# Decoder layer with routed experts: the low half of the hidden values is computed on VectorE for the second group's pairs of tiles

## The reference, cut to what matters

```python
shared = _swiglu(xf, sW1, sW2, sW3)
h = silu(einsum('td,efd->etf', xf, eW1)) * einsum('td,efd->etf', xf, eW3)
eo = einsum('etf,edf->etd', h, eW2)
specialist = einsum('te,etd->td', combine, eo)      # combine: two experts of eight per token
moe_out = (shared + specialist).reshape(B, S, d)
```

## Time and profile before

| | |
|---|---|
| median of 3 runs | 2320.03 us (2316.13 to 2321.22) |
| the profiled execution's own time | 2315.4 us |
| its span, first to last instruction | 2313.7 us |
| mean granted TensorE clock | 0.934 |
| busy: PE / DVE / ACT / POOL | 85% / 60% / 52% / 30% |
| experts' part | about 2040 to 2313.7 us |
| second group's pairs beside the gathers | about 2205 to 2282 us |

### The profile page before, as it was taken

One profiled execution on the slowest core, in us unless ns is written; L12 is line 12 of the kernel. 1 busy time (PEld: TensorE's weight loads), 2 busy tenths in 40 slices (PEclk: granted clock), 3 DMA queues, 4 the chain that ended last, 5 costly groups with the idle time before them and its releaser, 6 DMA issues. The chain is left out here.

```text
span 2313.7 us, 37956 instructions
## 1 busy us (share of the span) xinstructions
PE 1958.2 (85%) x13464; PEld 1002.0 (43%) x13464; DVE 1397.7 (60%) x3126; ACT 1194.2 (52%) x2157; POOL 699.9 (30%) x693
## 2 busy tenths in 40 slices
PE   4899999999999999967999999847888887459973
PEld 2556565655565656542333233212333333236642
DVE  5665656564656565526878777735677876513344
ACT  2554545454545454534777777743555664125541
POOL 2111101110111111122333333124466666412266
PEclk8999999999999999987999899977999998779996
DMA  5111111111111021123223222200011201133355
GB/s 155 46 40 34 38 37 37 37 38 38 37 32 43 20 46 29 37 63 57 56 56 56 37 50 55 32 18 28 1 37 38 65 28 37 39 101 104 105 161 155
DMA packets 97082, 122.82 MB, mean 53 GB/s; under 512 B 14305, under 2 KB 73985, under 8 KB 96897
## 3 DMA queue, kind: packets, MB, share of 16 engines
q1 hardware_dynamic: 79872, 93.11, 17.1%
q0 software_dynamic: 6144, 16.79, 2.3%
q10 hardware_dynamic: 10880, 10.49, 1.4%
HBM read 52.64 MB, written 33.82 MB: 37 GB/s over the span
## 5 line engine op out<-in xcount | busy, mean ns | idle before, releaser
L1037 DVE TENSOR_REDUCE x_NM<-x_pm 128x1 f32<-128x512 f32 x512 | 342.6, 687 | 108.4 <-PE x_pm L780 106.3
L962 ACT ACTIVATE x_PR<-x_pS 128x512 f32<-128x512 f32 x512 | 300.9, 601 | 115.6 <-PE x_pS L796 108.9
L309 PE MATMUL a_pa<-a_PR,a_V 128*128 128x512 f32 (+3 forms) x1024 | 340.7, 440 | 0.7 <-ACT a_PR L389 0.3
L389 ACT ACTIVATE a_PR<-a_pS 128x384 f32<-128x384 f32 (+1 forms) x384 | 201.4, 525 | 206.7 <-PE a_pS L298 204.3
L471 DVE CUSTOM_DVE_ANT_0 a_pm<-a_pm,a_causal 128x128 f32<-128x128 f32 (+3 forms) x512 | 247.2, 509 | 84.9 <-PE a_pm L284 70.1
L544 POOL CAST a_YT_hi<-a_Y 128x512 f16<-128x512 f32 x64 | 40.2, 628 | 759.1 <-DVE a_Y L479 759.1
L780 PE MATMUL x_pm<-x_KT,x_QT 48*128 48x512 f16 x512 | 198.6, 406 | 22.7 <-DMA x_QT<-q_k_parts 22.0
L796 PE MATMUL x_pS<-x_QT,x_KT 49*128 49x512 f16 x512 | 194.2, 396 | 17.3 <-ACT x_PR L962 16.1
L479 DVE TENSOR_TENSOR a_Y<-a_pa,a_RS 64x512 f32<-64x512 f32 x128 | 88.0, 688 | 181.0 <-ACT a_RS L397 179.8
L309 PEld LDWEIGHTS a_pa<-a_PR,a_V 128*128 128x128 f32 x1024 | 174.7, 192 | 29.8 <-ACT a_PR L389 11.3
L284 PE MATMUL a_pm<-a_KA,a_QA 128*128 128x128 f16 (+3 forms) x512 | 142.5, 308 | 44.9 <-DVE a_NM L471 27.9
(11 more groups left out here) (360 smaller groups left out, 4519.4 us busy)
## 6 DMA issues: line engine op xcount, KB each, us to landing
a_QA<-a_nat_q SPq DMA_DIRECT2D x128, 128.0 KB, 2.3
e_xr<-sent SPq DMA_DIRECT2D x80, 128.0 KB
made<-e_eo ACTq DMA_DIRECT2D x40, 256.0 KB
a_KA<-a_nat_k SPq DMA_DIRECT2D x64, 128.0 KB, 2.3
a_KB<-a_nat_k SPq DMA_DIRECT2D x64, 128.0 KB, 2.4
x_KT<-q_k_parts SPq DMA_DIRECT2D x48, 128.0 KB, 4.3
x_QT<-q_k_parts SPq DMA_DIRECT2D x48, 128.0 KB, 4.4
f_w_stage<-in_w SPq DMA_DIRECT2D x12, 512.0 KB
```

Of the source, the lines that this page charges most:

```text
L309: m = eng.matmul(pa[j % 2][:, P * kc:T], V[:, u % 2, kc, j, :], PR[:, i % 4, at:at + T - P * kc], start=(kc == 0), stop=(kc == TT - 1))
L389: eng.activation(PR[:, i % 4, 0:n], pS[i % 2][:, 0:n], ACT.Exp, scale=SCALE).then_inc(s_e, 1)
L962: eng.activation(PR[:, kc, j, :], pS[i % 2][:, :], ACT.Exp, scale=SCALE).then_inc(s_e, 1)
L1037: eng.tensor_reduce(NM[:, v % 2, c:c + 1], ring_bank("max", v, n)[:, :], AX.X, ALU.max, negate=True).then_inc(s_red, 1)
```

## The change

In the pairs of the second group (p from 28 to 39) `low` is taken from POOL's loop and put into DVE's, behind `hidden_out(p-1)` and in front of the additions. The first group's 28 pairs keep it on POOL. The waits of `low` and the semaphore it raises stay the same. The functions `side_by_side` and `Plan` are also moved to another place in the file, with no change in them.

```diff
 # vector_program
+        def low(p):
+            eng.wait_ge(s_hi, p + 1)
+            after(eng, s_ht, p - 1)
+            eng.tensor_tensor(H16[1][:, p % 2, :, :], TH[:, p % 2, :, :], H16[0][:, p % 2, :, :], ALU.subtract).then_inc(s_lo, 1)
+
...
                 activate(p)
             if 1 <= p <= NP:
                 hidden_out(p - 1)
+            if firsts[1] <= p < NP:
+                low(p)
             if p >= 2:
                 for i in returns_at(p - 2):
                     combine(i)
 # gpsimd_program
         for p in range(NP + 2):
-            if p < NP:
+            if p < firsts[1]:
                 low(p)
             if p >= 1:
                 for i in returns_at(p - 1):
                     gather(i)
```

More of the change, by code:

```diff
@@ L122, in low, with side_by_side, __init__, work_behind @@
                                  op0=ALU.mult, op1=ALU.subtract).then_inc(self.split_done, 1)
+def side_by_side(*threads):
+    at = [next(t, None) for t in threads]
+    while any(a is not None for a in at):
+        n = min((a, i) for i, a in enumerate(at) if a is not None)[1]
+        at[n] = next(threads[n], None)
+class Plan:
+    HOP = 0.2
+    WEIGHT = 0.01
+    def __init__(self, threads):
+        self.at, ended, free = {}, {}, {}
+        behind = self.work_behind(threads)
+        heads, begun = [0] * len(threads), [0.0] * len(threads)
+        while True:
+            ready = []
+            for i, steps in enumerate(threads):
+                if heads[i] < len(steps):
+                    name, before, passes = steps[heads[i]]
+                    if all(n in ended for n in before):
+                        t = max(begun[i], free.get(passes[0][0], 0.0), *(ended[n] for n in before))
+                        ready.append((t - self.WEIGHT * behind[name], t, i))
+            if not ready:
+                break
+            _, t, i = min(ready)
+            name, before, passes = threads[i][heads[i]]
+            begun[i] = t
+            for e, us in passes:
+                t = max(t, free.get(e, 0.0))
+                self.at.setdefault((e, name), t)
+                free[e] = t + us
+                t += us + self.HOP
+            ended[name] = t
+            heads[i] += 1
+        assert heads == [len(steps) for steps in threads]
+    def work_behind(self, threads):
+        own = {name: sum(us + self.HOP for _, us in passes) for steps in threads for name, _, passes in steps}
+        then = {name: [] for name in own}
+        for steps in threads:
+            for n, (name, before, _) in enumerate(steps):
+                for x in before:
+                    then[x].append((name, own[x]))
+                if n:
+                    then[steps[n - 1][0]].append((name, 0.0))
+        behind = {}
+        for first in own:
+            stack = [first]
+            while stack:
+                rest = [n for n, _ in then[stack[-1]] if n not in behind]
+                if rest:
+                    stack += rest
+                else:
+                    name = stack.pop()
+                    behind[name] = max([own[name]] + [behind[n] + us for n, us in then[name]])
+        return behind
@@ L1228, in cross_attention @@
         block.tensor(tensor_program)
[L1231 to L1295, removed]
 class Stage:
```

## The result

| | before | after |
|---|---|---|
| median, same chip | 2320.34 us (9 executions, 2316.13 to 2331.82) | 2336.1 us (9 executions, 2333.3 to 2348.2) |
| profiled execution's own time | 2315.4 us | 2335.06 us |
| first gather to the end of the span | 103.2 us | 120.3 us |

The ratio of the times is 1.0074, with a 95% interval of 1.005 to 1.0098. Forecast were 2312.8 us and a range of 2306.0 to 2318.5: the result lies outside, on the slow side. Executions of one kernel scatter by some 15 us, most of it upstream of the part that changed (in the traces kept, the first gather starts anywhere between 2201.9 and 2224.5 us).

What follows compares the result with a forecast made beforehand. Bound: the start of group 1's first gather at 2286.23, set by the store of pair 39. Gains 1.2 + 1.3 + 1.7 + 3.0 = 7.2 us took the 2320.03 us median to 2312.8, range 2306.0 to 2318.5.

Steps and rivals of the forecast that it cites:

- The failed step: Pairs beside the gathers: rows_out stays 1.42 us later than in the quiet cycle, so 6.53 us a pair against 6.71.
- (1): Start of the pairs beside the gathers: tanh(32) comes at 2221.9 in place of 2223.08, 1.2 us earlier.
- (2): Seven steps from the tanh of pair 32 to that of pair 39: 6.53 us each instead of 6.71, gaining 1.3 us.
- (3): Last pair: PE can take the low half 3.57 us after tanh instead of 5.28, gaining 1.7 us.
- (4): PE's clock in the last pair: 2.4 GHz through the 6.09 us from transposes to result copy, gaining 3.0 us, or 0.
- The third rival: Beside the gathers: denser gathers make signals to ACT's rows_out later; at 3.1 us lateness 4.6 us slower, 2324.6; chance 0.16.
- the first rival: Beside the gathers: late signals vanish with POOL's low half, steps near 5.15 us; gain 13.3 us, 2306.7 us; chance 0.2.
- The second rival: DVE's low half and POOL's gathers shut each other out; 3.6 us lost, gain only 3.6, 2316.4 us; chance 0.12.
- Its chain in the prediction: DVE's rows_out, high, low, additions, next activate: 6.65 us after tanh; behind a whole gather it passes 7.16 by about 0.45.

Runs made afterwards that it cites:

- e5_again: The changed kernel, unchanged, run again on chip 12 as control; ratio 0.9953 to the kernel before, 2305.73 us against 2318.89.
- e3_both: The kernel before, with VectorE doing the low-half subtraction a second time, into scratch, where the change puts it; chip 12, ratio 1.0015 to the kernel before.
- e1_spacer: The changed kernel plus one 1.16 us scratch subtraction on POOL before each set of gathers; chip 12, ratio 1.0012 to the kernel before.
- e18_fifth: The changed kernel, unchanged, on chip 14 as control; ratio 1.0088 to the kernel before, 118.3 us from first gather to the end.

## Why the prediction was wrong, and where it was right

**The failed step** is the one that I called a choice: the pairs' lateness beside the gathers is "1.42 us more than in the quiet cycle", "I keep its lateness", "since the gathers that go with it stay". The gathers stay in number, but not in density. POOL's low half was also the pause between them, and taking it away changed the very cause on which the lateness depends. In the terms of the sum: (1) had tanh(32) 1.2 us earlier, and it came 16.0 us later, counted from the first gather; (2) had 1.3 us gained in the seven steps, and 6.65 were lost; (3) and (4), 4.7 us together, brought 3.7. The text knew that POOL's road gets 13.5 us shorter and treated it only as a gain.

The sentence on which the choice leaned, that the loop "goes round without POOL's low half", doesn't fit the order of the streams either: on PE `turn_rows(p+1)` stands behind `turn_hidden(p-1)`, which needs `low(p-1)`. In the trace of before PE waits for it once in the seven steps:

```profile
2236.19 0.27 PE L2294 MATMUL e_pT<-id,e_H_hi 128*128 128x128 f16 x2 [1.31 <-POOL e_H_lo L2404]
...
2236.63 0.61 PE L2263 MATMUL e_pX<-id,e_xr 128*128 128x128 f16 x8
```

**The third rival** had the mechanism: denser gathers make PE's signals later. Its size was bounded by the largest lateness in the trace, 2.12 us, plus a guess of 3.1. Measured: a step of 26.6 us between the tanh of pairs 31 and 32 (11.3 before), and 7.67 us a step after it (53.65 / 7). Its price was 8.21 us a step, near the second number; the first has no counterpart in the trace of before, where never more than four gathers stood in a row while a low half was still to come. Its chance of 0.16 was too small, and its place was too narrow: not only ACT's wait for rows, but PE's own issue.

**On chip 12** the forecast's sum can be read term by term, since nothing crawls. The trace of before that it is set against is that of the first comparison; none was taken on chip 12. ACT's rows of e5_again:

```profile
2222.09 0.59 ACT L2333 ACTIVATE e_TH<-e_pH 128x512 f32<-128x512 f32 x1
...
2262.05 0.60 ACT L2333 ACTIVATE e_TH<-e_pH 128x512 f32<-128x512 f32 x1 [1.28 <-PE e_pH L2279]
...
2270.05 0.60 ACT L2344 ACTIVATE e_eo<-e_pO 128x512 f32<-128x512 f32 x1 [1.57 <-PE e_pO L2305]
```

- (1) The start: tanh(32) at 2222.09, forecast 2221.9; 0.9 us gained from the first gather on, forecast 1.2. Right.
- (2) The steps: 39.96 / 7 = 5.71 us, forecast 6.53. Too high: 7.0 us gained in place of 1.3. On the same chip a step takes 6.61 us with the low half on POOL (e3_both) and 6.38 with a subtraction on POOL that nothing waits for (e1_spacer), and in none of the three does a wait of ACT stand against "remote". That fits steps that go with POOL's road, as in the first rival, but without the late signals that this rival named.
- (3) The last pair and (4) the clock: from tanh to the copy of the result 8.00 us in place of 11.37, 3.4 us gained where 1.7 + 3.0 = 4.7 were forecast. The clock stayed at 1.00, 2.4 GHz, in the stretch of the last pair, as forecast.
- POOL's 48th gather over at 2272.4 (forecast "by 2273"), group 1's first at 2275.30 (forecast 2279), idle 2.92 us before it (forecast some 6).
- Sum: 10.9 us from the first gather on in place of 7.2, and 13.2 us between the medians. The ratio 0.9953 is inside the range as forecast (2306.0 and 2318.5 by 2320.03: 0.9940 to 0.9993), but in part by luck, with the largest gain in the term that was put at 1.3; it is the other chips that the range missed.

**What stayed right** in the changed kernel on every chip: the low half at 0.69 us on VectorE, the gathers 1.25 us apart, the additions at 2.07 us for four, and the last pair at full clock. From its tanh to its copy it takes 7.65 to 7.66 us on the chips that crawl, 8.00 on chip 12, in place of 11.37; the first profile's row, columns as above:

```profile
2294.15:2301.81 7.66, 5.11 (x52) 3.98 (x49) 6.47 (x13) 2.31 (x5) 2.84 (x3) 1.00 0.63 195
```

The second rival (low and gathers shut each other out) did not show: in the first profile low's longest is 755 ns and the longest gather 1.45 us. Its chain in the prediction adds up to 6.69 us, not 6.65, which changes nothing.

**What stays open.** Why chip 12 does not crawl and the others do; transfers are no faster there (SP's loads of `sent` land a median of 2.1 us after their issue in the changed kernel's first profile, 2.3 in e5_again's). What is shared between the issue on POOL and the streams of the other engines. It is not that instructions are loaded late: in the first profile no packet of the two instruction queues falls between 2212 and 2244, and PE's matmuls at 2240.60 and 2240.82 are close together again before the next one. And whether the crawl would be there in an execution of which no records are kept: all times here are of executions with records of span and clock. The Trainium skill, page "NOTIFIC — the notification-queue block", section "7.1 Overflow: three behaviours, one of which stalls the engine", says that the block that collects the engines' records holds a producer back when its own pipeline is full. No run here shows that this happened; steps of equal length on PE and signals that arrive late would fit it, but that is argued and not shown.

## What to carry to other kernels

An instruction on an engine that issues transfers is also a pause in its stream. Before it is moved away, ask what will then follow each other without a gap, and look for the longest row of that kind in the trace: where the trace has none, no row of it bounds the cost. And run the changed kernel once more as a control beside each set of experiments, on the same chip: here the first runs looked like a confirmation on a chip where the effect did not exist.

## What the runs showed of the hardware that was not expected

- On three of the four numbered chips, and in the first comparison, after ten to twelve indirect transfers issued 1.25 us apart TensorE falls to one instruction per 0.7 or 1.4 us, for some 15 us in the traces where 20 go in a row, and its signals reach ScalarE up to 20 us late (tanh(32), above); e18_fifth's stretch is the row below. On chip 15 a pause of 1.16 us after every four prevents it; on chip 3 one of about half that only puts it off, and one of 1.16 us after every eight does not help.
- It does not depend on the bytes: 16 a row or 1024 give F 118.2 and 118.3 us on one chip.
- POOL busy with memsets at the same pace brings no crawl (88.7 us on chip 14, where the gathers crawl).

```profile
2225.00:2241.00 16.00, 4.00 (x12) 1.08 (x10) 0.77 (x3) 1.23 (x3) 9.24 (x10) 0.50 0.32 90
```
